# A Mamba block with mixture of experts on one NeuronCore: logarithms of the step widths and the first block's input in PSUM, new slots for the side work

## What is computed

```python
h   = x @ W_base.T + b_base + LoRA(x, cond_8) * 2
for direction in (forward, reverse):                  # d = 512 inner channels, 16 states
    xi, z = split(h @ in_proj.T)
    xi  = silu(causal_conv4(xi) + conv_b)
    dt, B, C = split(xi @ x_proj.T)                    # 16, 16, 16
    dt  = softplus(dt @ dt_proj.T + dt_b)
    s_t = exp(dt_t * A) * s_{t-1} + dt_t * xi_t * B_t  # a scan over 1024 tokens, for each d and n
    y_t = sum_n s_t * C_t + D * xi_t
    out += (y * silu(z)) @ out_proj.T
x = x + out
x2 = x @ W2(cond_8).T + bias
x = x + MoE(x2)                                        # 8 experts, top 2, hidden 1024
```

## Time and profile before

| what | us |
|---|---|
| median of 3 runs | 1588.65 (1586.16 to 1588.87) |
| the profiled execution's own time | 1587.74 |
| its span | 1585.9 |
| TensorE busy | 1342.3 (85%) |
| VectorE busy | 1010.7 (64%) |
| GpSimd busy | 982.7 (62%) |
| ScalarE busy | 740.4 (47%) |

### The profile page before, as it was taken

One profiled execution on the slowest core, in us unless ns is written; L12 is line 12 of the kernel. 1 busy time (PEld: TensorE's weight loads), 2 busy tenths in 40 slices (PEclk: granted clock), 3 DMA queues, 4 the chain that ended last, 5 costly groups with the idle time before them and its releaser, 6 DMA issues. The chain is left out here.

```text
span 1585.9 us, 16391 instructions
## 1 busy us (share of the span) xinstructions
PE 1342.3 (85%) x5214; PEld 784.3 (49%) x5214; DVE 1010.7 (64%) x1171; ACT 740.4 (47%) x1263; POOL 982.7 (62%) x486
## 2 busy tenths in 40 slices
PE   6778798688887778889877677888899999999997
PEld 3223233233232333333332222343699999999996
DVE  3498889988899888788888888986511111111110
ACT  4667666658766357686553664434021111111111
POOL 0488888898888878689898978895022222222221
PEclk9799999999999889999987987989699999999999
DMA  4335444434344344334443434442478988988983
GB/s 153 111 131 160 127 138 135 134 128 137 107 145 163 122 143 139 106 125 144 147 152 115 150 106 140 155 150 70 182 280 312 318 318 312 327 309 311 330 303 85
DMA packets 103143, 282.44 MB, mean 178 GB/s; under 512 B 9249, under 2 KB 19106, under 8 KB 87570
## 3 DMA queue, kind: packets, MB, share of 16 engines
q1 hardware_dynamic: 95570, 271.17, 49.3%
q0 software_dynamic: 7488, 10.23, 3.0%
HBM read 271.40 MB, written 9.96 MB: 177 GB/s over the span
## 5 line engine op out<-in xcount | busy, mean ns | idle before, releaser
L400 PE MATMUL ps_y<-arena,ident 128*128 128x512 f32 x1024 | 545.1, 665 | 168.3 <-POOL arena L1083 152.5
L1083 POOL TENSOR_TENSOR arena<-arena 128x1024 f32<-128x1024 f32 x213 | 505.9, 2375 | 157.2 <-DVE arena L836 151.0
L400 PEld LDWEIGHTS ps_y<-arena,ident 128*128 128x128 f32 x1024 | 197.9, 206 | 474.3 <-POOL arena L1083 251.3
L1069 POOL TENSOR_TENSOR arena<-arena 128x1024 f32<-128x1024 f32 x128 | 306.0, 2391 | 1.3
L1111 POOL DMA_INDIRECT out_x<-arena x39 | 61.8, 1585 | 317.3 <-ACT arena L769 260.2
L644 ACT ACTIVATE ps_de<-arena,An 128x512 f32<-128x512 f32 x256 | 175.2, 684 | 133.6 <-DVE arena L833 132.3
L833 DVE TENSOR_TENSOR_SCAN arena<-ps_de,arena 128x512 f32<-128x512 f32 x128 | 155.8, 1217 | 65.3 <-ACT arena L644 32.4
L820 DVE TENSOR_TENSOR ps_u<-ps_du,arena 128x512 f32<-128x512 f32 x256 | 178.5, 697 | 21.3 <-DVE arena L847 5.6
L833 DVE TENSOR_TENSOR_SCAN arena<-ps_de,hlast,arena 128x512 f32<-128x512 f32 x128 | 163.5, 1277 | 41.7 <-POOL arena L1069 25.8
L644 ACT ACTIVATE arena<-arena,An 128x512 f32<-128x512 f32 x256 | 181.1, 707 | 0.0
L1041 DVE TENSOR_TENSOR arena<-ps_du,arena 128x512 f32<-128x512 f32 x39 | 27.0, 692 | 231.2 <-PE ps_du L524 231.2
(11 more groups left out here) (219 smaller groups left out, 1494.5 us busy)
## 6 DMA issues: line engine op xcount, KB each, us to landing
arena<-bc_scratch SPq DMA_DIRECT2D x256, 512.0 KB, 4.6
arena<-in_W SPq DMA_DIRECT2D x117, 1024.0 KB, 9.4
arena<-in_xT SPq DMA_DIRECT2D x2, 1024.0 KB, 6.5
arena<-in_w2c SPq DMA_DIRECT2D x1, 2048.0 KB, 9.3
arena<-in_xT SPq DMA_DIRECT2D x4, 512.0 KB, 6.1
X_scratch<-stg SPq DMA_DIRECT2D x12, 128.0 KB, 4.5
out_x<-stg SPq DMA_DIRECT2D x12, 128.0 KB, 4.8
ipT<-in_ipT SPq DMA_DIRECT2D x1, 1024.0 KB, 7.4
```

The source lines that it names most:

```text
L400: t = e.matmul(Y[j][:, :], ident[:, :], hc[:, i % NP, j, :], start=False, stop=(n == 15))
L1069: e.tensor_tensor(uA[:, turn % 2, :, :], duA.rearrange("p (o t) -> p o t", o=1).to_broadcast([128, 2, TH]), ring[:, turn % NR, 0, :, :], A ...
L1083: e.tensor_tensor(hc[:, i % NP, :, :], hh[:, i % NH, :, :], c, ALU.mult).then_inc(gp_hc, 1)
```

## The change

1. **Logarithms in PSUM.** Ln now writes a spare bank instead of `sc1`. TensorE's program reserves the bank in unit g + 4 (`leave`, no instruction), ScalarE waits until its last reader is done (`is_left`), VectorE's step width reads it and frees it. Ln comes last in ScalarE's unit g + 4 instead of ahead of diagonals and Silu.
2. **First input through PSUM.** At a block start TensorE copies x of the even group into `ps_du` with an identity matrix (`input_again`), once the last u of the block before has been read; VectorE's `du` multiplies it there by dt, in place.
3. **Order at a block start.** `scans` is split into `scan_2` (odd group) and `scan_1` (even group). VectorE's order in the first unit of a block becomes scan_2, du, u, scan_1.
4. **Slots.** The tables of step widths, convolutions, rows, second weights, conditioning, input projection, gates, output projection and tiles have new numbers. While tiles run, side work has only `ps6` in a shorter time (g to g + 4 instead of g - 4 to g + 4), and in units 6 to 17 instead of 0 to 13 for the second weights.

```diff
-    STEP_AT |= {at(q_, 12 + 8 * w): (q_, 1, w) for w in range(2)}
-        STEP_AT |= {at(q_, 44 + 12 * w): (q_ + 1, 0, w) for w in range(2)}
-CONV_FROM, ROWS_FROM = [14, 2, 14], [38, 28, 38]
+STEP_AT = {1: (0, 0, 1), at(0, 22): (0, 1, 0), at(0, 30): (0, 1, 1), at(0, 44): (1, 0, 0), at(0, 56): (1, 0, 1),
+           at(1, 12): (1, 1, 0), at(1, 20): (1, 1, 1), at(1, 44): (2, 0, 0), at(1, 49): (2, 0, 1),
+           at(2, 18): (2, 1, 0), at(2, 26): (2, 1, 1), at(2, 47): (3, 0, 0), at(2, 53): (3, 0, 1),
+           at(3, 12): (3, 1, 0), at(3, 20): (3, 1, 1)}
+    (14, 17, 20, 23, 27, 30, 35, 38), (2, 5, 8, 11, 17, 20, 25, 28), (17, 20, 23, 26, 31, 34, 37, 40)))
-X1_AT = {41: 0, 43: 1}
-IN_AT = {45 + 2 * k: (k // 2, k % 2) for k in range(8)}
+X1_AT = {45: 0, 46: 1}
+IN_AT = {48 + 2 * k: (k // 2, k % 2) for k in range(8)}
...
+            def leave(name, banks):
+
+                p = min(banks, key=lambda c: taken[c])
+                taken[p] = len(place) + 1
+                turns[p] += 1
+                place[name] = (p, turns[p])
...
+            def input_again(i):
+                q, th, pr, n = unit(i)
+                has_x(e, q, 2 * pr, th)
+                if i:
+                    e.wait_ge(dv_u, i)
+                e.matmul(DU[:, :], ident[:, :], xc[q % 2][:, 2 * pr, HB[th]], start=True, stop=True).then_inc(pe_xc, 1)
...
             for i in range(NU + LAG):
+                if i < NU and i % 16 == 0:
+                    input_again(i)
...
-                tiles_on = any(g - 4 <= i <= g + 4 for g in TILE_AT)
-                side = [6] if i < 14 or tiles_on else both_side
+                tiles_on = any(g <= i <= g + 4 for g in TILE_AT)
+                side = [6] if 6 <= i < 18 or tiles_on else both_side
+                if i - 4 in STEP_AT:
+                    q, th, pr = STEP_AT[i - 4]
+                    for j in range(2):
+                        leave(("ln", q, th, 2 * pr + j), side)
...
-                    e.activation(sc1[:, j, :], sc1[:, j, :], ACT.Ln, bias=1.0).then_inc(ac_sp, 1)
+                    p = is_left(e, ("ln", q, th, 2 * pr + j))
+                    e.activation(PS[p][:, :], sc1[:, j, :], ACT.Ln, bias=1.0).then_inc(full[p], 1)
...
-                e.scalar_tensor_tensor(w, w, 0.0, sc1[:, m % 2, :], ALU.max, ALU.add).then_inc(dv_dt, 1)
+                e.scalar_tensor_tensor(w, w, 0.0, PS[p][:, :], ALU.max, ALU.add).then_inc(freed[p], 1)
...
-                e.tensor_tensor(DU[:, :], dt[:, width_at(q, th, 2 * pr), :], xc[q % 2][:, 2 * pr, HB[th]],
-                                ALU.mult).then_inc(dv_du, 1)
+                is_read(e, ("ln", q, th, 2 * pr))
+                e.wait_ge(pe_xc, i // 16 + 1)
+                e.tensor_tensor(DU[:, :], DU[:, :], dt[:, width_at(q, th, 2 * pr), :], ALU.mult).then_inc(dv_du, 1)
...
-                if i < NU and i % 16 == 0:
-                    du(i)
                 if i < NU:
-                    u(i)
-                    scans(i)
+                    if i % 16 == 0:
+                        scan_2(i)
+                        du(i)
+                        u(i)
+                    else:
+                        u(i)
+                        scan_2(i)
+                    scan_1(i)
```

More of the change, by code:

```diff
@@ L189, in build @@
         dv_bss, pe_wm, dv_wm, dv_An, ac_A, gp_dz, gp_pad = (sem(n) for n in ("bss", "pwm", "wm", "An", "A", "dz", "pad"))
-        ac_cv0, dv_cv, ac_xc, ac_cd, ac_sp, dv_dt = (sem(n) for n in ("cv0", "cv", "xc", "cd", "sp", "dt"))
+        ac_cv0, dv_cv, ac_xc, ac_cd, ac_sp = (sem(n) for n in ("cv0", "cv", "xc", "cd", "sp"))
         ac_dA, dv_du, gp_du, dv_u, gp_u, dv_sA, dv_sB, ac_hl, gp_hc, pe_y = (
             sem(n) for n in ("dA", "du", "gdu", "u", "gu_", "sA", "sB", "hl", "hc", "y"))
-        dv_hc, dv_hl = sem("dhc"), sem("dhl")
+        dv_hc, dv_hl, pe_xc = sem("dhc"), sem("dhl"), sem("pxc")
         ac_dgD, pe_D, ac_ev, dv_fl = (sem(n) for n in ("dgD", "D", "ev", "fl"))
@@ L245, in tile_buffers @@
             return 2 + i, sX, sB, sT
+        blocks = [(q, th, m) for q in range(NQ) for th in range(2) for m in range(4)]
         place, turns, taken, early_turns = {}, [0] * 8, [0] * 8, []
@@ L257, in is_read, with is_left @@
             e.wait_ge(freed[p], k)
+        def is_left(e, name):
+            p, k = place[name]
+            e.wait_ge(freed[p], k - 1)
+            return p
         blk = ctx.enter_context(nc.Block())
@@ L425, in _ @@
                 step_width(0, 0, m, early)
+            for m in range(2):
+                leave(("ln", 0, 0, m), [6, 7])
             early_turns.extend(turns)
             taken[:] = [0] * 8
-            for p in range(2):
+            for p in range(3):
                 e.wait_ge(freed[p], turns[p])
             for i in range(NU + LAG):
+                if i < NU and i % 16 == 0:
+                    input_again(i)
                 if i >= LAG:
@@ L608, in step_width @@
                 if k >= 2:
-                    e.wait_ge(dv_dt, k - 1)
+                    is_full(e, ("ln", *blocks[k - 2]))
                 e.activation(sc1[:, m % 2, :], w, ACT.Abs).then_inc(ac_sp, 1)
@@ L636, in decay @@
                 if n == 0:
-                    e.wait_ge(dv_dt, 8 * q + 4 * th + 2 * pr + 2)
+                    for j in range(2):
+                        is_read(e, ("ln", q, th, 2 * pr + j))
                 for j in (1, 0):
@@ L742, in _ @@
                     tile_T(*TILE_AT[i - 3])
+                if i - 4 in STEP_AT:
+                    step_ln(*STEP_AT[i - 4])
             gate(*GATE_AT[NU - 1])
@@ L820, in u, with scan_2 @@
                 e.tensor_tensor(U[:, :], DU[:, :], ring[:, turn % NR, 0, i % 2, :], ALU.mult).then_inc(dv_u, 1)
-            def scans(i):
+            def scan_2(i):
                 q, th, pr, n = unit(i)
@@ L834, in scans, with scan_1 @@
                                      hlast[:, 2 * pr + 1, n:n + 1] if th else 0.0, ALU.mult, ALU.add).then_inc(dv_sA, 1)
+            def scan_1(i):
+                q, th, pr, n = unit(i)
                 e.wait_ge(dv_u, i + 1)
@@ L917, in _ @@
                         step_width(q, th, 2 * pr + j)
-                if i in (5, 11):
-                    second_weights(i // 11)
+                if i in (11, 17):
+                    second_weights(i // 17)
                 if i in YG_AT:
@@ L1055, in du @@
                 m = 2 * pr + 1
-                e.wait_ge(dv_dt, 8 * q + 4 * th + m + 1)
+                is_read(e, ("ln", q, th, m))
                 has_x(e, q, m, th)
```

37 lines of the change are left out of this document (14 added, 23 removed).

## The result

| | before | after |
|---|---|---|
| median of 4 runs each, us | 1588.76 (1586.16 to 1590.73) | 1606.04 (1605.63 to 1606.91) |
| ratio, 95% interval | | 1.011 (1.0093 to 1.0128) |
| span of the profiled execution, us | 1585.9 | 1605.1 |

The change made the kernel slower by 1.1%, 17.3 us. The forecast was 1575.0 with a range of 1559 to 1598, so it had the wrong sign, and the result lies outside the range. It is 4 us from the rival that lets the banks decide (1602).

A forecast was written before the change was run, and what follows sets the result against it. The scan stage was taken as bound by a dependency loop among VectorE, GpSimd and ScalarE, no engine full. Terms -33.4 - 4.8 + 21.6 + 3 = -13.6 gave 1574.1 us profiled, 1575.0 from the median; range 1559 to 1598.

The forecast's parts named there:

- the rival that lets the banks decide: TensorE stands at a taken bank, with an add and then the decay queued behind; slower, 1602 us, chance 0.18.
- +2.4 (conditioning): Conditioning products at units 45 and 46 come behind a step width product whose bank they need: 2.4 us slower.
- +6.5 (units 146 to 151): Units 146 to 151: ScalarE loads Silu, applies it, loads Ln, takes two and reloads Exp in one unit; +6.5 us.
- unit 48 chain: Input projection of unit 48 waits for the first step width; add, evacuation and unit 50's decay queue behind: 5.6 us.
- "third": At units 27, 35, 61, 89, 113 and 159 a bank is taken one or two units after the logarithms: +6.5 us.
- Step widths, -33.4: VectorE's step widths (L796), one input now in PSUM, fall from 1792 ns to 0.64 to 0.67 us each: -33.4 us.
- First input, -4.8: At block starts, GpSimd's L1069 behind L809 falls from 2.67 to 2.36 us with one input in PSUM: -4.8 us.
- Order at a block start, +21.6: du and u now stand between VectorE's first scan and the one releasing GpSimd's product: 1.35 x 16 = +21.6 us.
- Slots, relief, -18: New table parts step widths from output blocks, gates or tiles at units 122 to 125, 131 to 134, 143 to 146, 215 to 217: -18 us.
- signs of "right": Step widths 0.64 to 0.67 us; L1069 2.36 at block starts; pairs there about 9.9; decay wait at unit 50 5 or more.
- one of "wrong": Step widths over 1 us; block starts at 8.9; or waits for ScalarE's decays under 35 us or over 70, against 46.2.

## Why the prediction was wrong, point by point

The runs part the sum into three steps, each with the terms of the prediction that belong to it. Each measured step is a difference of two ratios, in us of 1589, and can be off by some 4 us:

| step | run reached | predicted | measured |
|---|---|---|---|
| new slots, no bank held: -18, +2.4 (conditioning), +6.5 (units 146 to 151) | 1.0005 | -9.1 | +1 |
| input copy and order at block starts on top (and Ln last in its unit) | 1.0024 | +16.8 | +3 |
| logarithms in PSUM: -33.4 for the step widths, +5.6 (unit 48 chain) and +6.5 ("third") for held banks | 1.011 | -21.3 | +14 |

**The step that failed** is the price of the held banks. The prediction put it at 12.1 us; the third step gives 14 + 32 = 46, and freeing the banks one unit earlier takes 42 off. On the first step the prediction was 10 us too hopeful, on the second 14 too gloomy, and these two nearly cancel, which is luck. The held banks alone turned the sign.

**Step widths, -33.4.** Right: 0.673 us each in PSUM, 32 to 34 us less of VectorE's time, and with the banks freed early nearly all of it reaches the kernel (1593.6 to 1564.4). The Trainium skill (SBUF — State Buffer, SBUF: two separate sides) says that a VectorE instruction with two SBUF inputs and a GpSimd instruction that reads SBUF exclude each other for a whole instruction. The trace agrees: 1792 ns with both inputs in SBUF, 673 with one in PSUM.

**First input, -4.8.** Half right. Clean block starts fall by 0.33 us, but alone the copy gains nothing; the longest wait for it is 7.1 us at unit 144, behind the output block, and pairs 24 and 152 lose more. I had that case only as a remark on the range. With the new slots and order VectorE waits 2.7 us for it in all, and its use is in the du between the scans.

**Order at a block start, +21.6.** Right in its mechanism: the pair takes 7.17 + 2.8 = 10.0 us (I had 9.9), undoing it in the change gives 16.4, and alone it costs 23. Together with the input, the two terms were +16.8, or 1.05 for each block start, and the eight clean ones rose by 0.9 to 1.2 each. But on top of the new slots both edits cost only 3 us (1.0005 to 1.0024; 5 by the medians, 6 in the traces). There the clean block starts rise by 0.9 to 1.1 too, and the one at unit 32 by 4.3, while pairs 158 (2.8), 70 (2.2), 18 (1.5) and 34 (1.3) get shorter. The term's price depends on what else is late, and I had it fixed.

**Slots, relief, -18.** The places were right and gave about 23, some of it step widths that only moved. I looked for new meetings of side work only at units 48 and 146 to 151, and priced those as +8 and +6.5. With no bank held, pair 48 is 4.3 us longer (I had 2.4), where a scan waits 4.88 us for a decay that stands behind the conditioning products; pair 148 is 4.4 longer, and 158, 112, 70 and 14, which I had not named, 5.0, 2.8, 2.2 and 2.2. So relief and new lateness cancel, where I had -9.1.

**Slots, unit 48 chain, 5.6 of the +8.** Right in every link, too small in size: the scan of unit 50 waits 8.42 us, and TensorE's low clock in it is what I had left out. Moving the projections by one unit takes the pair at unit 50 from 9.7 us over the loop to 1.2, and that at 62, where the last projection meets the next pair of logarithms, from 4.8 to 0.5.

**Slots, "third, at units 27, 35, 61, 89, 113 and 159 ... about 1 each".** This is the term of the failed step that was furthest off. Measured by the earlier step width, a taker one or two units behind a pair of logarithms costs 3 to 5.5 us, at 27, 35, 61, 81, 89, 113, 151 and 159. The six that I named make 25.5 us instead of 6.5, and 81, 151 and 119 (a finished tile, 2.0), which are not in the term, another 10.4. I had argued that convolutions have two units of room. But the room belongs to the product's second half, and that half sits in TensorE's queue behind the add; the first half starts after the wait and, in all six such places, at the lower clock; and Silu then holds the decay behind it. The row for this was in my own list, L351 at 6.72 us. I used it for the rival only, and did not carry it into the sum.

**Chances.** The rival had the mechanism, its place and nearly its size (1602). It got 0.18, on the argument above. With 3 to 5 us for each taker in place of 1, the third term is 18 to 30 instead of 6.5, and the sum -2 to +10: the sign would have been open. That the rival's 1602 came within 4 us is in part luck, for it kept the slots' relief and the order's full price, and their errors nearly cancel.

**What would show it.** The four signs of "right" appeared (step widths of 0.67, GpSimd's L1069 of 2.36 us at block starts, the pair of 10.0, the wait at unit 50), together with one of "wrong", and that one decided: decay waits of 89.2 us, over 70.

## To carry to other kernels

Putting a value in a shared bank gives the bank's next taker a new releaser. Before costing the shorter instruction, list who takes that bank next in an in-order queue, what stands behind it, and when the new releaser runs; here it ran one unit too late, and one number (g + 4 for g + 5) turned +17 us into -27. And a term has no fixed price: the same order cost 23 us alone, 16 in the change, 7 once the banks came free early, and with the copy 3 on top of the slots. A wait in such a queue can cost more than itself, since its successors are in order too and, in nine of ten such waits here, ran at the lower clock behind it.

## What was not expected of the hardware

- A held TensorE can pay twice. At unit 48 it idles 7.16 us, the clock falls from 1.00 to 0.50 meanwhile, and then four passes take 3.75 us, where four take 1.88 at full clock.
- The length of one wait alone does not tell the clock behind it. A wait of 3.51 us in the change ended at the lower level, where the clock already was after an earlier one of 3.98; in the kernel with the early step widths a wait of 3.54 us (unit 61) began and ended at full clock.
- The same edit has different prices in different company. The input copy is worth 0 in the kernel before, costs 9 us or more without step widths, and is worth about 1 us for each block start once du stands between the scans; the slots are worth 0 in the kernel before and 15 us in the kernel with the copy and without VectorE's step widths.
